# Second output projection and feed-forward part by halves of fp32r in a two-layer transformer kernel

## What is computed

```
mod = (silu(c) @ wmod)            # 6 vectors: sa, ca, ga, sb, cb, gb
h = layernorm(x) * (1 + ca) + sa;  x = x + ga * attn(h)
h = layernorm(x) * (1 + cb) + sb;  x = x + gb * ffn(h)
```

## Time and profile before

| what | value |
|---|---|
| median of 3 runs | 1065.32 us (1061.94 to 1069.73) |
| profiled execution, time | 1066.8 us |
| profiled execution, span | 1065.0 us |
| mean granted TensorE clock | 0.966 |
| busy: TensorE, VectorE, ScalarE, GpSimd | 998.2, 776.8, 580.1, 288.9 us |
| feed-forward part of layer 0, first tile to last matmul of down(1) | 446.5 to 530.2 us |
| attention of layer 1, its turns | about 550 to 832 us |
| second output projection on TensorE | 832.1 to 897.7 us, with hooked steps |

### The profile page before, as it was taken

The page is one execution under the profiler, slowest core; times in us unless marked ns, Lnnn a source line. Parts: engine busy times, 40 slices in busy tenths (PEclk is TensorE's granted clock), DMA queues, the critical chain, the costliest instruction groups (busy, mean ns, idle before and its releaser), DMA issues.

```text
span 1065.0 us, 17345 instructions
## 1 busy us (share of the span) xinstructions
PE 998.2 (94%) x5864; PEld 796.6 (75%) x5864; DVE 776.8 (73%) x1351; ACT 580.1 (54%) x1153; POOL 288.9 (27%) x246
## 2 busy tenths in 40 slices
PE   7999999999999999999979999999997999659996
PEld 5778988898889854454459898989896545449995
DVE  4789999899989858983358777787877125638774
ACT  2567878887878687830136555555655012326651
POOL 1034234423442320130021212112110003536772
PEclk8999999999999999998989999999998999879998
DMA  7098777877876851160001101010100202547856
GB/s 230 2 234 169 175 161 156 171 170 155 167 164 159 243 111 49 70 177 0 1 32 58 58 31 59 30 59 30 59 0 1 74 1 95 220 147 226 246 163 212
DMA packets 82480, 121.59 MB, mean 114 GB/s; under 512 B 26099, under 2 KB 59646, under 8 KB 81792
## 3 DMA queue, kind: packets, MB, share of 16 engines
q1 hardware_dynamic: 70368, 86.88, 26.9%
q0 software_dynamic: 12032, 34.11, 16.2%
q10 hardware_dynamic: 32, 0.00, 0.0%
HBM read 70.28 MB, written 38.04 MB: 102 GB/s over the span
## 4 chain that ended last, share of the span: by engine, by line
PE 77%; DVE 11%; ACT 4%; issue 3%; DMA 3%; POOL 2%; POOLq 0%; ACTq 0%; DVEq 0%; SPq 0%
PE psum L690 11%; PE psum L691 11%; PE psum L692 11%; PE psum L916 5%; PE psum L1060 5%; PE psum L744 5%; PE psum L941 3%; PE psum L863 3%; PE psum L733 3%; PE psum L822 3%; PE psum L803 3%; PE psum L1113 2%; PE psum L872 2%; DVE arena L1580 2%; PE psum L668 1%
## 5 line engine op out<-in xcount | busy, mean ns | idle before, releaser
L1580 DVE SCALAR_TENSOR_TENSOR arena<-arena,par_in 128x1024 f32<-128x1024 f32 x144 | 183.4, 1283 | 32.7 <-ACT arena L1189 23.0
L690 PE MATMUL psum<-G_r,arena_r 128*128 128x512 f32 x320 | 132.8, 415 | 4.6 <-DVE G_r L1673 4.1
L691 PE MATMUL psum<-G_r,arena_r 128*128 128x512 f32 x320 | 128.0, 400 | 0.0
L692 PE MATMUL psum<-G_r,arena_r 128*128 128x512 f32 x320 | 127.7, 399 | 0.0
L690 PE MATMUL psum<-arena_r 128*128 128x256 f32 x384 | 117.8, 307 | 2.9 <-DVE arena_r L1763 1.5
L691 PE MATMUL psum<-arena_r 128*128 128x256 f32 x384 | 110.7, 288 | 0.0
L692 PE MATMUL psum<-arena_r 128*128 128x256 f32 x384 | 110.6, 288 | 0.0
L2040 POOL DMA_DIRECT2D arena<-arena x64 | 53.8, 983 | 206.8 <-DVE arena L1592 206.6
L1337 ACT ACTIVATE arena<-psum,small 128x256 f32<-128x256 f32 x128 | 59.3, 472 | 87.3 <-DVE small L1738 87.3
L1179 ACT ACTIVATE arena<-psum 128x1024 f32<-128x1024 f32 x48 | 49.3, 1026 | 62.2 <-PE psum L692 61.7
L2056 POOL TENSOR_TENSOR arena_r<-arena,arena_r 128x512 fp32r<-128x512 f32 x16 | 20.7, 1294 | 214.6 <-ACT arena_r L1306 214.6
(11 more groups left out here) (243 smaller groups left out, 2340.6 us busy)
## 6 DMA issues: line engine op xcount, KB each, us to landing
arena<-arena POOLq DMA_DIRECT2D x64, 256.0 KB, 5.7
slot_rows<-nowhere SPq DMA_DIRECT2D x16, 576.0 KB, 4.5
G<-in_w_moe SPq DMA_DIRECT2D x24, 384.0 KB, 8.9
arena<-slot_rows SPq DMA_DIRECT2D x32, 288.0 KB, 3.2
arena<-bands SPq DMA_DIRECT2D x16, 528.0 KB, 4.2
sq_rows<-arena POOLq DMA_DIRECT2D x16, 512.0 KB, 7.8
arena<-in_w_qkvz SPq DMA_DIRECT2D x16, 384.0 KB, 4.0
arena<-in_qkv_codes SPq DMA_DIRECT2D x16, 384.0 KB, 3.2
```

What stands on the lines that cost most here:

```text
L690: nc.tensor.matmul(dst, w_l, x_h, start=start, stop=False, skip_group_check=True)
L691: nc.tensor.matmul(dst, w_h, x_l, start=False, stop=False, skip_group_check=True)
L692: return nc.tensor.matmul(dst, w_h, x_h, start=False, stop=stop, skip_group_check=True)
L1580: nc.vector.scalar_tensor_tensor(by_batch(dst), by_batch(u[s])[:, :, j:j + S], par_in[:, bass.ds(M_CW + (w * H + h) * TAPS + j, 1)], by_ba ...
```

## The change

- Feed-forward part of layer 0: tiles 2 to 5 of half 0, all of half 1, and both `down` go by halves. Tiles 0 and 1 of half 0 stay in full. New ScalarE copies: `upper_x`, `upper_gate_up`, `upper_down`, `upper_h`; new VectorE subtractions: `lower_x`, `lower_gate_up`, `lower_down`, `lower_h`. Both queues get a new order: `attn_half(1)` ahead of chunk 10, chunks 11 and 12 later, and `gate_up(0, 3)` no longer waits for a product.
- SP: the codes of head 0 are loaded after all gate/up tiles, those of head 1 directly after; the output projection's weights after `down(1)`.
- GpSimd: `weights_out(p)`, eight multiplications of 512 columns instead of one of 4096, each between `weights(h)` and `weights_lower(h)` of heads 2 to 9.
- Second output projection: head by head, with both m inside; heads 0 to 11 of half 0 and 0 to 6 of half 1 by halves, the others in full. The weights' halves are made at the end of the last turn, those of the heads' outputs as TensorE goes. The hooks get new positions.
- Tiles of fp32r are allocated in several pieces in place of one (`twice`), at the same place.

```diff
@@ SP
-            sp.wait_ge(sg("a0_gT"), H)
-            load1(0)
             sp.wait_ge(sg("attn_out"), 2 * KC)
             sp.dma_start(wmod[1], a["wmod1"])...
+            sp.wait_ge(sg("f_u"), 2 * MT)
+            load1(0)
+            sp.wait_ge(sg("a1_wmul"), 1)
+            load1(1)
+            sp.wait_ge(sg("f_down"), 2 * KC)
             sp.dma_start(wo_c, a["wo_codes"])...
@@ TensorE, gate_up
-                if s >= 2:
+                if s >= 2 and s != 3:
                     pe.wait_ge(sg("f_h"), s - 1)
+                if not full:
+                    pe.wait_ge(*at("f_x_lo", KC * (n + 1)))
+                    pe.wait_ge(*at("f_w_lo", f_w_hi_at(m)))
...
+                            i = by_halves(ffn_bank(n, m, up)[0:r, :], wg_h[:, w], lut_w_r[:, w], part(xf[n][0], k), part(xf[n][1], k),
+                                          k == 0, k == KC - 1)
@@ TensorE, second projection
-            pe.wait_ge(sg("a1_womul"), 1)
+            pe.wait_ge(sg("a1_womul"), H // 2)
             pe.wait_ge(sg("a1_o_sb"), H)
...
+            first_half = {4: ..., 9: ..., 14: ..., 18: ..., 22: ..., 26: ..., 31: ...}
             for n in range(2):
+                for h in range(H):
+                    if h < OH2[n]:
+                        pe.wait_ge(*of_out("o_lo", KC + 1 + n * OH + h + 1))
+                    for m in range(KC):
...
+                            i = by_halves(bank(2 * m + n), wo_h[:, c], wo_l[:, c], o_hi[o_slot[n][h]], o_part(halves, h, n), h == 0, False)
...
+                        if n and KC * h + m in first_half:
@@ ScalarE, order of the first half
+            lut_act(7) lut_act(8) lut_act(9) upper_x(0) upper_gate_up(2) upper_gate_up(3) lut_act(10)
+            silu_f(0, 0) upper_gate_up(4) silu_f(0, 1) upper_h(0, 0) upper_gate_up(5) part_square_act(n1b)
+            silu_f(0, 2) upper_h(0, 1) silu_f(0, 3) lut_act(11) upper_h(0, 2) silu_f(0, 4) upper_h(0, 3)
+            lut_act(12) upper_down() silu_f(0, 5) upper_h(0, 4) upper_h(0, 5) upper_gate_up(0) upper_gate_up(1) upper_x(1)
@@ ScalarE, after the last turn
+            for p in range(KC + 1):
+                nc.scalar.activation(wo_h[:, p * T:(p + 1) * T], wo_c[:, p * T:(p + 1) * T], ACT.Copy)...
@@ VectorE, order of the first half
             lut_dve(9)
+            lower_x(0) attn_half(1) lower_gate_up(2) lut_dve(10) lower_gate_up(3) product_f(0, 0) part_centre(n1b)
+            product_f(0, 1) lower_h(0, 0) lower_gate_up(4) product_f(0, 2) lower_gate_up(5) product_f(0, 3) lut_dve(11)
+            lower_h(0, 1) part_stat(n1b) lower_h(0, 2) product_f(0, 4) part_diag(n1b) lut_dve(12) lower_h(0, 3)
+            lower_down() product_f(0, 5) lower_h(0, 4) lower_h(0, 5) part_modulate(n1b)
+            lower_gate_up(0) lower_x(1) lower_gate_up(1) modulation(1) ffn_half(0)
@@ GpSimd
-            nc.gpsimd.tensor_tensor(wo_c, wo_c, wo_s, ALU.mult).then_inc(sg("a1_womul"), 1)
...
+            def weights_out(p):
+                c = bass.ds(p * 2 * D, 2 * D)
+                nc.gpsimd.tensor_tensor(wo_c[:, c], wo_c[:, c], wo_s[:, c], ALU.mult).then_inc(sg("a1_womul"), 1)
+            pool.wait_ge(sg("in_wo"), 80)
+            with pool.Fori(1, H // 4 + 1) as i:
+                for par in range(2):
+                    weights(2 * i + par, par)
+                    weights_out(2 * i + par - 2)
+                    weights_lower(2 * i + par, par)
```

More of the change, by code:

```diff
@@ L123, in sb, with twice @@
         return ctx.enter_context(nc.sbuf_tensor(name, [P, cols], dt))[:, :]
-    def twice(name, cols):
-        with nc.sbuf_tensor(name, [P, cols], F32) as t:
+    def twice(name, *ends):
+        with nc.sbuf_tensor(name, [P, ends[-1]], F32) as t:
             plain = t[:, :]
-        return plain, sb(name + "_r", cols, F32R)
+        return plain, *[sb(f"{name}_r{i}", e - b, F32R) for i, (b, e) in enumerate(zip((0, *ends), ends))]
     with ctx:
@@ L174, in build @@
         ARENA = 24832
-        arena, arena_r = twice("arena", ARENA)
+        UPPER = 3 * (B * (S + PAD)) + 9 * T + TAPS + 3 * BAND
+        ends = (5 * T, UPPER, 20 * T, ARENA)
+        arena, *arena_r = twice("arena", *ends)
         def carve(*sizes, base=0, of=arena):
@@ L179, in carve @@
             for n in sizes:
-                v.append(of[:, o:o + n])
+                if of is not arena:
+                    i = sum(o >= e for e in ends)
+                    b = (0, *ends)[i]
+                    assert o + n <= ends[i], (o, n)
+                    v.append(arena_r[i][:, o - b:o - b + n])
+                else:
+                    v.append(of[:, o:o + n])
                 o += n
@@ L209, in build @@
         rb, sq_in = swq, swk
+        (wg_h,) = carve(2 * UPC, base=UPPER, of=arena_r)
+        wd_h, wd_l = halves[:, 10 * T + 512:12 * T], lut_w_r[:, 2 * UPC:LUTC]
+        xf = [[halves[:, 0:T], halves[:, T:2 * T]], [halves[:, 2 * T:3 * T], halves[:, 3 * T:4 * T]]]
+        hsb_h = carve(*[512] * MT, base=at_w, of=arena_r)
+        (hsb_l,) = carve(MT * 512, base=3 * UW + 3 * T, of=arena_r)
+        in_full = (0, 1)
+        split_order = [m for m in range(MT) if m not in in_full] + list(in_full)
         (wout,) = carve(H * D, base=at_w)
@@ L1308, in _ @@
             silu_f(0, 0)
+            upper_gate_up(4)
+            silu_f(0, 1)
+            upper_h(0, 0)
+            upper_gate_up(5)
+            part_square_act(act, "n1b", fc, fsq)
+            silu_f(0, 2)
+            upper_h(0, 1)
+            silu_f(0, 3)
             lut_act(11)
-            silu_f(0, 1)
+            upper_h(0, 2)
+            silu_f(0, 4)
+            upper_h(0, 3)
             lut_act(12)
[L1312 to L1317, removed]
+            upper_down()
+            silu_f(0, 5)
+            upper_h(0, 4)
+            upper_h(0, 5)
+            upper_gate_up(0)
+            upper_gate_up(1)
+            upper_x(1)
+            silu_f(1, 0)
+            silu_f(1, 1)
+            upper_h(1, 0)
+            silu_f(1, 2)
+            upper_h(1, 1)
             part_square_act(act, "n2a", gc, gsq)
@@ L1727, in _, with out_lower @@
             lower_in(1)
+            def out_lower(n, h):
+                dve.wait_ge(*of_out("o_hi", KC + 1 + n * OH + h + 1))
+                nc.vector.tensor_tensor(o_part(halves, h, n), o_part(G, h, n), o_hi[o_slot[n][h]].bitcast(F32), ALU.subtract)\
+                    .then_inc(of_out("o_lo", 0)[0], 1)
             def turn1(h, hh, par, st):
@@ L1794, in _ @@
             turns1(dve, turn1)
+            for h in range(1, OH):
+                out_lower(0, h)
             for k in range(KC):
@@ L1812, in _ @@
             dve.wait_ge(sg("mod"), 12)
+            for h in range(OH2[1]):
+                out_lower(1, h)
             link, step = sg("moe_link"), [0]
```

175 lines of the change are left out of this document (141 added, 34 removed), and 3 rows, old and new, of the table REUSED.

## The result

The changed kernel takes 1060.1 us (median of 6, 1057.3 to 1064.1), the one before 1066.0 beside it: ratio 0.9941, 95% interval 0.9918 to 0.9963. That is 6 us less, inside 1%, where 8.2 were forecast. Measured again in a later group the ratio was 0.9952 (0.9927 to 0.9977).

A forecast was written before the change was run, and what follows sets the result against it. TensorE, busy 94% of the span, was taken as the bound. Feed-forward -10.1, attention +5.5 and projection -3.6 sum to -8.2 us: 1057.1 us against the median of 1065.3, range 1049.5 to 1065.5.

The forecast's parts named there:

- Feed-forward, first half: Four tiles by halves save 2.6 us, a new 1.7 wait, modulation 2.4 earlier; with down(0) saving 1.9, running sum 4.3.
- Worth nothing: The 8.84 us GpSimd multiplication leaving the feed-forward part gains nothing: it blocked VectorE for 7.99 us, but behind the modulation.
- Second half: Feed-forward, second half: six tiles by halves save 3.9 us and down(1) 1.9, bringing the part's sum to 10.1.
- Moved loads: Head 0's later loads and weight preparation are done at T + 9, TensorE wants them at T + 9.6: hidden, 0.6 us spare.
- The sum: All terms: -10.1 + 5.5 - 3.6 = -8.2 us, giving 1057.1 us against the median.
- Attention: Eight added GpSimd multiplications of 1.31 us block a two-column VectorE operation and lengthen eight turns: 5.5 us cost, bounds 0 and 10.5.
- about 1 us: Sign to look for in the attention: eight L1738 of this length, with turns of 17.8 us instead of 17.1.
- Rival A: In the attention VectorE gets in first and the multiplications cost nothing: -13.7, 1051.6 us; chance 0.25.
- Projection: Second output projection by halves: gain 3.6 us, bounds 0 and 6.1, as VectorE's chain moves by 3.6 only.
- the seven heads of half 1 do little beyond keeping the hooks early: In the projection, the last matmul comes 7 us earlier but VectorE's chain moves by 3.6 only.
- Rival C: Longer waits in the attention turns lower the granted clock: slower than before, 1069 us, or 1081 with twice the stretch; chance 0.07.
- Rival B: The first feed-forward half is fed late by VectorE and ScalarE: five of 10.1 us lost, 1062 us; chance 0.20.

The follow-up runs named there:

- experiment 7: The changed kernel with the feed-forward part run in full fp32 again, its splits out and the changed orders kept: 1067.6 us, ratio 0.9998 to before.
- experiment 1: The changed kernel with each of the eight GpSimd multiplications of the output weights scaling 2 columns instead of 512: 1081.9 us, ratio 0.9894 to before.
- experiment 4: The changed kernel with the half 0 hooks moved up inside the projection of half 1, to groups 1, 4, 6, 10, 13, 15, 19: 1082.3 us, ratio 0.9884.
- experiment 8: The kernel of experiment 6 with product(0,0) also ahead of lower_gate_up(3) in VectorE's order: 1050.5 us, ratio 0.9856 to before.
- experiment 9: The changed kernel with only the last hook of half 1, the spread of n4a, moved from group 31 to 28: 1058.1 us, ratio 0.9922 to before.
- experiment 2: The changed kernel with each GpSimd multiplication of the output weights held back until the turn's probabilities are normed: 1083.2 us, ratio 0.990 to before.
- experiment 3: The changed kernel with the second output projection in full fp32, head by head with its hooks, splits out: 1092.3 us, ratio 0.9983 to before.
- experiment 6: The changed kernel with the edits of experiment 2 and experiment 4 together: 1049.3 us, ratio 0.9833 to before.
- experiment 10: The kernel of experiment 3 with the last hook back at group 28: a single execution, 1057.1 us.
- experiment 5: The changed kernel again, unaltered, in a later group: 1059.6 us, ratio 0.9952 to before.

## Why the prediction was right, and where not

**Feed-forward, first half: right in place and nearly in size.** Wait before (0,2): 1.54 for 1.7. Modulation 2.4 us earlier: it began 23.55 us after the part's start (472.47 - 448.92) against 25.86, 2.3 less. The part gained 12.1 us in the first profile and 10.5 in the second, for 10.1 forecast; what lies between the two is the modulation's 1.6. From the spread behind the modulation to the end of the part both profiles take 41.5 us, before 50.0: 8.5 less, for 7.7 forecast. With the 2.3 ahead of it that is 10.8, and the length of the modulation itself adds 1.3 in the first profile and takes 0.3 away in the second. "Worth nothing", my price for the GpSimd multiplication that leaves this part, stands as far as this goes; it was not tried by itself.

**Second half: right.** From its first tile to the end of the part pass 29.8 us (490.66 to 520.5) instead of 36.0 (494.23 to 530.2), 6.1 less for 5.8 forecast. All tiles and down by halves together, the new wait taken off, gained 8.8 us for 8.7 (experiment 7).

**Moved loads: too kind, by up to 1 us.** 0.6 to spare was forecast, and 0.46 of waiting seen in the first profile. There GpSimd's `weights` took 2.33 instead of 1.85 (at 516.48, beside a VectorE tensor_tensor with both inputs in SBUF), and its lower half waited another 0.74 for ScalarE's copy. In the second profile `weights` took 1.91 and TensorE didn't wait. The other kernels with this part by halves split the same way: 0.45 to 0.46 of waiting where `weights` took 2.2 to 2.4 us (experiments 1, 4, 8 and 9), none where it took 1.8 to 1.9 or 2.1 (2, 3, 6 and 10). The sum had no term for this.

**Attention: right, mechanism and size.** 5.5 was forecast; the two profiles give 5.9 and 4.5. The difference between them lies behind the turns: the 15 turns take 262.5 us in both, and 257.4 in experiments 1 and 2, so the block costs 5.1. The other 1.1 above before's 256.3 is not the block, and I had no term for it. L1913 is stretched once for each of the eight multiplications, to 0.61 to 1.22 us, 0.9 in the mean for the "about 1 us" of my list, and these turns are at 17.9. The Trainium skill, "SBUF — State Buffer", section "Who interferes with whom", says that a tensor_scalar with operands in SBUF can take the pair of ports that VectorE shares with GpSimd, and that an instruction with at most one SBUF input, outside those modes, doesn't contend. By that rule, the trace agrees: L1913 was stretched, L1931 with one SBUF stream and one from PSUM stayed at 1.28 with GpSimd beside it. Rival A (multiplications cost nothing) fell: VectorE did not get in first.

**Projection: the right number, with a wrong reading, and a cost left out.** -3.6 was forecast to the residual add and the mean, -3.65 measured. Token half 0 took 23.2 us (829.08 to 852.28) for 23.7, and the walk through the hooks put the spread of n4a 58.6 us after the start, where it came at 58.5. But "the seven heads of half 1 do little beyond keeping the hooks early" misses that this is their whole worth: TensorE waits nowhere between the start and the mean, so the halves gave all their 6.2 us (experiment 3), 2.3 of them from the 14 groups of half 1, and the hooks' later places took 2.6 back. VectorE wasn't the bound: it waited 4.05 us for the counts. And I left out what TensorE does after the last hook. It stands behind the last matmul now, so TensorE idles for the 4.83 us that VectorE takes, the clock falls, and 1.5 to 1.8 us go. That is the step that failed: net 2.2 instead of 3.6.

**The sum.** By stages of the two profiles: feed-forward part -12.1 and -10.5, attention +5.9 and +4.5, projection to the centring -2.2 and -1.9 (67.9 and 68.2 for 70.1): -8.4 and -7.9, beside the -8.2 of the forecast. That these agree is partly luck: the feed-forward part gave more than forecast in the first profile, the projection 1.4 to 1.7 less in both, and the attention of the second profile cost 1 less. The first profile also shows the feed-forward part starting 2.4 us later, 0.7 more between it and the attention, and 2.5 more from the centring to the end of the span (165.3 for 162.8): its span is only 2.7 us shorter than before's. In the second profile the start is 0.8 earlier, the stretch between 0.5 longer and the end 0.9 longer (163.7), and the span 7.3 shorter. So the stages that the change touches don't hold these differences, 0.46 of the stretch between in the first profile excepted. The ratios say 5 to 6 us with some 2.5 either way: 8 is inside the interval of one of the two measurements (down to 0.9918, 8.7 us) and just outside the other's (0.9927, 7.8 us). Whether 2 us are missing is open.

Rival C fell: the clock stays 1.00 in the turns with the longer wait. It fell at another place, of which no rival spoke. Rival B (fed late) took no place either: 1.54 us of waiting between 446 and 480.

## What to carry to other kernels

A short operation on the shared path pays in full for a long one of the other engine beside it: place GpSimd's work next to VectorE operations that read PSUM, by a wait if need be (1.3 us a turn cost 5.1 us over eight turns in one place and nothing in the other). When matmuls get shorter or their order changes, the places of steps hooked in among them have to be worked out anew, and each must leave enough matmuls behind it to cover what VectorE does next. A stage whose number comes out right can still hide two errors: a gain of 6.2 and a loss of 2.6 looked like the forecast 3.6.

## What the runs showed of the hardware

- The granted clock at the mean of n3b. In all six profiles in which TensorE idled 4.8 us ahead of it (the changed kernel's two, experiments 1, 2, 3 and 7), the mean took 3.4 to 3.8 us instead of 2.0; in the four in which it waited 2.25 us or not at all there, and at no hook (before, experiments 4, 6 and 8), 1.98 or 1.99. Waits of 1.55 and 2.25 us close together gave one of each (experiments 9 and 10), with the same DMA traffic beside the mean, so the length of the idle time alone doesn't say on which side it falls.
- A 128x512 step by halves takes 0.70 us against 0.865 in full, and the 38 replaced in the projection saved 6.2 us: 0.163 each, as worked out from the steps.
- On one chip every kernel took longer, before's by 2.5% (1093.2 for 1066.3), with the same times up to the end of the second projection. Behind it the four kernels of that group took 188.9 to 193.1 us from the centring to the end of the span, where 162.6 to 165.3 pass in the eight profiles from elsewhere. In all four, ScalarE's first activation behind the variance matmuls of n3b (L450) came 2.1 to 5.6 us after them, in the changed kernel 0.04; that is a part of it at most, and why wasn't tried.
- The same 48 four-column passes of one kernel took 6.5 us in one execution and 8.1 in another (experiment 5), at a mean granted clock of 0.81 and 0.64. In every profile the clock fell from 1.00 while these passes ran.
- Of the eight stretched two-column operations none was over 1.22 us, and each ended within 0.03 us of the end of GpSimd's multiplication: what a short operation pays is what is left of the long one when it starts.
